# A three-part layer on one core: the prologue in halves with its gate work spread over attention steps, and the first delta-rule head's first stage put ahead of the expert tiles

## The chip, the cores and the metric

One core of one Trainium2 chip runs the whole layer in one launch. The metric is the device time of one execution in microseconds (us). All arithmetic is fp32. The core's engines are PE (matrix multiplies and transposes), DVE and ACT (elementwise work; ACT also has exp, ln and silu, whose tables are loaded when the function changes), POOL (elementwise work and indirect DMAs) and SP, which here only issues DMAs. Each engine runs its own instruction list in order, and they meet through semaphores.

## The reference

Input x has 1024 rows of 256 (two batches of 512). Two branches read the same normalised rows, and both are added to x:

```
xn  = layernorm(x)
out = x + delta(xn) + ffn(xn)

ffn:    h = rmsnorm(xn) * ln1; 16 causal attention heads of 128; hid = xn + attention @ o_w
        x2 = rmsnorm(hid) * ln2; 16 experts, the best 4 for each row, weighted, plus one shared expert
delta:  qkvz = xn @ W_qkvz; ba = xn @ W_ba            (16 key heads, 32 value heads)
        q, k, v = silu(causal convolution of 4 taps); q, k normalised by their lengths
        beta = sigmoid(b);  g = -exp(A_log) * softplus(a + dt_bias);  G = running sum of g in a chunk
        per head: decay = exp(G_i - G_j) below the diagonal; solve a unit triangular system
        from (k k^T) * decay * beta; scan over the chunks; gate with silu(z), rmsnorm, @ W_out
```

## The kernel before

The kernel runs in four sections, in this order on every engine.

**Prologue** (L422 to L480 are SP's and PE's ends of it, L1098 to L1131 ACT's, L1422 to L1470 DVE's). SP loads x in two DMAs that count into one semaphore, and DVE waits for both (L1423). DVE takes the statistics of the eight row tiles (L1424, L1426); ACT takes one square root, DVE a reciprocal, and DVE writes the eight tiles of `xn` (L1431). ACT squares and sums the eight tiles (L1105) and takes a second root (L1107), then copies the transposed rows into `xnT` (L1110). DVE writes the eight scaled tiles `xr` (L1436). PE transposes `xn` (L476), multiplies `xnT` with `W_ba` in 32 small products (L482), transposes `xr` (L489), and DVE copies that to `xrT` with the factor ln1 (L1441). Then the gate work, a chain between DVE, ACT and PE: DVE L1446 to L1450, ACT L1120 to L1124 (exp and ln), DVE L1452 to L1456, PE's sums over a chunk (L573, L574), DVE L1468 and L1470, eight transposes (L577), and ACT's four operations L1127 to L1131, which make `growT` and `erowT`. Mixed into it is the first pair of attention heads: the projections of q and k (L505) and of v (L520). PE starts the scores (L530) only when the gate's sums are there.

**Attention.** 16 steps (eight pairs of heads, twice for the two batches), written out so that PE always has the next pair's projections to do: a step k is v(k), the first two parts of q and k for k+1, transposes of the probabilities of head 0, a third part, transposes for head 1, a fourth, the products with v for both heads (L609), the scores of k+1 for head 0, the output product (L631), the scores for head 1. DVE masks and finds the maxima (L1487, L1489), ACT takes the exponentials (L1157), DVE scales them (L1625). Routing work of the first batch already sits in steps 9, 10 and 12 in the same way, between the two products with v. SP clears 2 MB of the table of rows in each of the first eight steps. `send_rows(0)` on POOL (L1980) scatters the first batch's rows at the end of step 12.

**Shared and routed experts.** PE does six blocks of the shared expert's gate and up products (L647) and six of its down products (L658), DVE the routing in between, and `slots()` (L1589 to L1598) says which tile of 128 rows goes to which expert. POOL scatters the second batch's rows, then adds `hid` to `total` (L1988). Then 47 tiles ("slots") pass one after the other: load the rows, transpose (L684), gate and up (L699), silu and product (L1201, L1674), transpose (L711), down (L720), store. At the end all four engines meet in `section_end` (L270 to L273).

**Delta rule.** After the meeting SP loads the constants and the first weights (L363 to L369), and POOL clears four buffers (L2059 to L2064); PE, ACT and DVE wait for that (L1000, L1345, L1871). The loop over h runs from -2 to 15. Round h holds the scan of head h, the middle stage of head n = h+1 (its triangular system, its values and gates) and the first stage of head f = h+2: keys and queries projected (L749, L759), the convolution's first tap on ACT (L1226) and the other three on DVE (L1704), silu and squares (L1232 to L1249), their sums on PE (L771), lengths and scales on DVE (L1724 to L1739), and the decay table `dec` (SP's rows L376, POOL L1997, L2003 and L2011, ACT L1308). Round -2 has only the first stage of head 0. Round -1 has the first stage of head 1 and the middle stage of head 0, which begins with products of keys (L781) and `MT` (L1748), goes through DRAM (L392 to L401), and solves 16 rows on DVE (L1838 to L1848).

Of the kernel before, what the change touches and what calls it, by code (L numbers as in the profile page):

```python
# [29 lines left out]
RING = 6  # L30
TURN, LOGIT, PLACE = 9, 10, 12
# [12 lines left out]
def build(nc, d, out, debug=None):  # L44
# [9 lines left out]
    with ExitStack() as ctx:  # L54
# [13 lines left out]
        eps6 = sb("eps6", [P, 1])  # L68
        answer = sb("answer", [P, NT, TOPK], mybir.dt.uint32)
        pick = sb("pick", [P, NT, TOPK])  # L70
        yg = sb("yg", [P, 4, H])

# [22 lines left out]
        sd = early("sd", [P, NT])  # L95
        rstd = early("rstd", [P, NT])
        ssq = early("ssq", [P, NT])
        rms = early("rms", [P, NT])
        rrms = early("rrms", [P, NT])
        junk = early("junk", [P, H])  # L100
        eps5 = early("eps5", [P, 1])
        ba = early("ba", [P, NT, 2 * NV])
        ga = early("ga", [P, NT, NV])
        gb = early("gb", [P, NT, NV])
        gc = early("gc", [P, NT, NV])
        gs = early("gs", [P, NT, NV])
        g = early("g", [P, NT, NV])
        G = early("G", [P, NT, NV])

        wqk = early("wqk", [P, 2, HK, 2 * P])  # L110
        wv = early("wv", [P, HK, 2 * P])
        wo = early("wo", [P, 2, H])
# [11 lines left out]
        cmp_b = early("cmp_b", [P, 4, E, E])  # L124
# [40 lines left out]
        w13 = early("w13", [P, SHT, HK, 2 * P])  # L165
        w2 = early("w2", [P, SHT, H])
        sg = early("sg", [P, 2, 512])
        xs = x2[:, 0:RING, :]
        xsT = xrT[:, 0, 0:3 * HK * P].rearrange("p (s k n) -> p s k n", s=3, k=HK)
        sgs = xrT[:, 1, 0:2 * I].rearrange("p (s n) -> p s n", s=2)  # L170
        hs = xrT[:, 1, 2 * I:4 * I].rearrange("p (s n) -> p s n", s=2)
        hsT = early("hsT", [IH, 2, 2, P])
# [17 lines left out]
        gkq = sb("gkq", [P, HK, 2 * D])  # L190
# [4 lines left out]
        cw = sb("cw", [P, NK, 4, TAPS])  # L195
        e_neg = sb("e_neg", [P, P])
        ones = sb("ones", [P, BL])
        cv = sb("cv", [P, 3, B, S])
        kT = sb("kT", [P, 2, NT, P])
        qT = sb("qT", [P, NT, P])  # L200
        sqb = sb("sqb", [P, R, NT, P])
# [3 lines left out]
        dec = sb("dec", [P, R, NT, P])  # L205
# [20 lines left out]
        sst = sb("sst", [P, U, BL])  # L226
        kq2 = sb("kq2", [P, 2, U])
        rk2 = sb("rk2", [P, NT])
        cb = sb("cb", [P, R, 2, NT])
        half = sb("half", [P, 2, U])  # L230
        nk2 = sb("nk2", [P, 2, NT])
        epsq = sb("epsq", [P, 3, NT])
        sxt = sb("sxt", [P, U, BL])
        sxv = sb("sxv", [P, R, NT])
# [44 lines left out]
        def _(sp):  # L279
# [73 lines left out]
            for s in range(RING):  # L353
                load_rows(s)
# [1811 lines left out]
```

## Time and profile before

| | us |
|---|---|
| median of 3 runs | 1630.26 (1629.26 to 1636.0) |
| the profiled execution | 1629.19 |
| its span, first to last instruction | 1627.4 |

| engine | busy us | share of the span |
|---|---|---|
| PE, matrix multiplies | 1534.4 | 94% |
| DVE | 1111.6 | 68% |
| ACT | 784.7 | 48% |
| POOL | 438.4 | 27% |

Busy shares are averages over the whole span. A step inside one section is judged from that section's own rows: who waits there, and for what. "<-" names the releaser of a wait, and times are counted from the span's start.

### The profile page before, as it was taken

To read this page: it belongs to the slowest core of one execution; us is meant where nothing else is said; L and a number is where in the kernel's file an instruction comes from. 1 tells how busy PE (TensorE), PEld (TensorE's weight loads), DVE (VectorE), ACT (ScalarE), POOL (GpSimd) and SP (SyncE) were. 2 spreads that over 40 slices of the span, in tenths; PEclk is the share of its full clock that TensorE was granted. 3 is DMA by queue.
4 is the path that set the end of the run, shared out by engine and by line. 5 is a ranking of instruction groups with operands and counts; after the bars stand their busy time and mean duration, and the time that the engine had idled before them with its cause. 6 is when DMAs were issued, how large, how long until landed. Compare 5 with 4: busy or idle time off the path is not lost.

```text
span 1627.4 us, 29153 instructions
## 1 busy us (share of the span) xinstructions
PE 1534.4 (94%) x10922; PEld 1081.3 (66%) x10922; DVE 1111.6 (68%) x2442; ACT 784.7 (48%) x1692; POOL 438.4 (27%) x277
## 2 busy tenths in 40 slices
PE   4999999999978995699999999999999999999987
PEld 3666666766656773376677677667668668667756
DVE  4544445465362333769889889988988988888875
ACT  3444345343413433445646645646555565564641
POOL 0000000003031005226335344444532531532410
PEclk8999999999998997889999999999999999999999
DMA  3234333223323323323234144143233223323201
GB/s 97 82 116 143 131 115 104 62 70 117 87 99 108 107 85 119 90 63 82 60 99 91 46 103 103 42 100 98 60 72 82 64 65 84 69 57 88 59 11 33
DMA packets 225051, 136.88 MB, mean 84 GB/s; under 512 B 160976, under 2 KB 196304, under 8 KB 224912
## 3 DMA queue, kind: packets, MB, share of 16 engines
q1 hardware_dynamic: 221840, 126.62, 28.6%
q0 software_dynamic: 3072, 8.39, 1.6%
q8 instruction: 89, 1.46, 0.4%
q14 instruction: 50, 0.41, 0.1%
HBM read 94.85 MB, written 35.91 MB: 80 GB/s over the span
## 4 chain that ended last, share of the span: by engine, by line
PE 80%; issue 10%; DVE 5%; ACT 2%; POOL 1%; DMA 1%; POOLq 1%; SPq 0%; ACTq 0%; DVEq 0%
PE ps L912 7%; PE ps L811 7%; PE ps L505 6%; PE ps L830 6%; PE ps L609 4%; PE ps L530 4%; PE ps L631 3%; PE ps L520 3%; PE ps L749 3%; PE ps L851 3%; PE ps L882 3%; PE ps L759 3%; PE ps L861 2%; PE ps L881 2%; PE ps L838 2%
## 5 line engine op out<-in xcount | busy, mean ns | idle before, releaser
L1279 ACT ACTIVATE vs<-ps 128x256 f32<-128x256 f32 x128 | 49.1, 383 | 258.0 <-PE ps L851 253.7
L2027 POOL TENSOR_TENSOR qg<-qT,Ebc 128x1024 f32<-128x1024 f32 x32 | 74.9, 2360 | 357.2 <-PE ps L882 357.2
L1704 DVE SCALAR_TENSOR_TENSOR cv<-ps,cw,cv 128x1022 f32<-128x1022 f32 (+2 forms) x96 | 122.6, 1279 | 28.0 <-ACT cv L1226 24.2
L912 PE MATMUL ps<-wout,xT 128*128 128x256 f32 x512 | 128.8, 396 | 2.2 <-DVE total L1814 2.2
L811 PE MATMUL ps<-xnT,gv 128*128 128x512 f32 x256 | 120.4, 614 | 10.6 <-DVE cv L1704 10.1
L1487 DVE TENSOR_TENSOR ps<-ps,causal_neg 128x128 f32<-128x128 f32 x128 | 37.4, 292 | 131.8 <-PE ps L530 131.8
L1715 DVE SCALAR_TENSOR_TENSOR cv<-ps,cw,cv 128x1022 f32<-128x1022 f32 (+2 forms) x96 | 122.6, 1277 | 5.5 <-ACT cv L1258 3.1
L1814 DVE SCALAR_TENSOR_TENSOR total<-ps,rr,total 128x256 f32<-128x256 f32 x256 | 119.0, 481 | 9.8 <-POOL rr L2033 3.0
L830 PE MATMUL ps<-xnT,gz 128*128 128x512 f32 x256 | 122.8, 604 | 2.6 <-DVE MT L1748 2.4
L505 PE MATMUL ps<-xrT,wqk 128*128 128x512 f32 x256 | 119.5, 601 | 3.6 <-ACT we L1116 2.8
L1157 ACT ACTIVATE we<-ps,bias 128x128 f32<-128x128 f32 (+3 forms) x128 | 65.7, 525 | 106.0 <-DVE bias L1491 106.0
L912 PEld LDWEIGHTS ps<-wout,xT 128*128 128x128 f32 x512 | 93.3, 192 | 28.2 <-issue 12.6
L2011 POOL TENSOR_TENSOR dec<-dec,cb 128x1024 f32<-128x1024 f32 x32 | 60.0, 1896 | 165.5 <-DVE cb L1737 134.5
L811 PEld LDWEIGHTS ps<-xnT,gv 128*128 128x128 f32 x256 | 47.1, 194 | 84.5 <-issue 71.5
L882 PE MATMUL ps<-AT,vs 128*128 128x128 f32 x512 | 91.2, 275 | 0.0
L1969 POOL TENSOR_SCALAR mean<-ssq 128x4 f32<-128x4 f32 x2 | 0.4, 192 | 307.9 <-ACT junk L1141 307.9
L851 PEld LDWEIGHTS ps<-vs,PT 128*128 128x128 f32 x512 | 65.9, 192 | 26.1 <-issue 15.7
L1226 ACT ACTIVATE cv<-ps,cw 128x1024 f32<-128x1024 f32 x32 | 35.6, 1114 | 94.0 <-PE ps L759 62.0
L1997 POOL TENSOR_TENSOR dec<-dec,e_neg 128x1024 f32<-128x1024 f32 x32 | 75.3, 2372 | 15.6 <-DMA dec<-grow_dram 15.6
L505 PEld LDWEIGHTS ps<-xrT,wqk 128*128 128x128 f32 x256 | 46.7, 193 | 45.9 <-issue 40.3
L1782 DVE SCALAR_TENSOR_TENSOR St<-St,eg,ps 128x128 f32<-128x128 f32 x128 | 35.9, 342 | 57.0 <-PE ps L861 57.0
L881 PE MATMUL ps<-qg,St 128*128 128x128 f32 x384 | 74.4, 275 | 0.0
(256 smaller groups left out, 3612.4 us busy)
## 6 DMA issues: line engine op xcount, KB each, us to landing
xs_dram<-zeros SPq DMA_DIRECT2D x16, 1024.0 KB, 6.4
dec<-grow_dram SPq DMA_DIRECT2D x32, 512.0 KB, 4.8
Ebc<-erow_dram SPq DMA_DIRECT2D x32, 512.0 KB, 5.0
wqk<-in_wqk SPq DMA_DIRECT2D x16, 512.0 KB, 3.6
xn<-xs_dram SPq DMA_DIRECT2D x47, 128.0 KB, 2.1
ys_dram<-yg SPq DMA_DIRECT2D x47, 128.0 KB, 1.9
we<-in_we SPq DMA_DIRECT2D x16, 352.0 KB
wv<-in_wv SPq DMA_DIRECT2D x16, 256.0 KB, 3.3
```

Source lines behind the costliest of these rows:

```text
L505: last = mm(ps[:, 6 + j % 2, :], wqk[:, i, c, w * P:(w + 1) * P], xrT[:, c, at:at + S], start=(c == 0), stop=(c == HK - 1))
L811: last = mm(ps[:, (Y, X)[r] + b, :], gv[:, k, r * D:(r + 1) * D], xnT[:, k, b * S:(b + 1) * S], start=(k == 0), stop=(k == HK - 1))
L830: last = mm(ps[:, X + b, :], gz[:, k, r * D:(r + 1) * D], xnT[:, k, b * S:(b + 1) * S], start=(k == 0), stop=(k == HK - 1))
L851: last = mm(ps[:, b, r * D:(r + 1) * D], PT[:, r * NT + 4 * b + m, :], vs[:, r, 4 * b + m, :], start=True, stop=True)
L881: mm(dst, St[:, m % 2, b * R + r, :], qg[:, r, t, :], start=True, stop=False)
L882: last = mm(dst, vs[:, r, t, :], AT[:, h % 2, r, t, :], start=(m == 0), stop=True)
L912: last = mm(ps[:, output_bank(t), r * H:(r + 1) * H], xT[:, r, t * P:(t + 1) * P], wout[:, r, :], start=True, stop=True)
L1704: ins = stt(row, pair(bank)[:, :, 0:S - k], cw[:, f, i, TAPS - 1 - k:TAPS - k], row, ALU.mult, ALU.add)
L1715: ins = stt(row, pair(bank)[:, :, 0:S - k], cw[:, n, 2 + r, TAPS - 1 - k:TAPS - k], row, ALU.mult, ALU.add)
L1814: ins = stt(total[:, t, :], ps[:, output_bank(t), r * H:(r + 1) * H], rr2[:, r, t:t + 1], total[:, t, :], ALU.mult, ALU.add)
L1997: tt(dec[:, r], dec[:, r], e_neg[:].unsqueeze(1).broadcast_to([P, NT, P]), ALU.add).then_inc(fl["g_self"], 1)
L2027: tt(qg[:, r], qT[:], Ebc[:, r], ALU.mult).then_inc(fl["g_qg"], 1)
```

## The change

It has two parts, in one kernel.

**Part one, the prologue.** x's two halves have semaphores of their own, and each half is normalised by itself. The square roots and reciprocals become a power of -0.5 on POOL over four numbers at a time; the mean square of `xn` is computed from the variance (three small DVE operations) in place of ACT's eight squares. `xr` of the first half is turned first, and the first q and k projections follow; the second half's transposes come between them and the next two projections. DVE and ACT share the copies to `xrT`. v(0) moves into step 0. All gate work leaves the prologue: the products with `W_ba` go into step 1 between the two products with v, DVE's and ACT's parts at the end of steps 1 and 2, the sums into step 3, the transposes and the tables into step 4. `growT` is now copied by DVE and `erowT` is taken from it. SP stores both tables in step 5.

**Part two, the first stage of head 0.** `cw`, `e_neg` and head 0's key weights are loaded in the prologue. `dec` of head 0 is loaded in step 6, masked by POOL behind `send_rows(0)`, and its exponential stands on ACT behind step 13. Keys and queries are projected after the last gate and up block (into banks 0 to 3), ahead of the last three down blocks; ACT's and DVE's work on them stands between the shared expert and the slots, `key_squares(0)` ahead of the first slot's transposes, `scaled_decays(0)` and `key_norms(0)` on POOL behind its addition to `total`. The delta-rule loop starts at h = -1. The wait for the cleared buffers is left to SP's `blocks_back(0)`. Some buffers share memory with others than before.

```
@@ SP
-            for i in range(2):
-                dma(total[:, 4 * i:4 * i + 4, :], xv[:, 4 * i:4 * i + 4, :]).then_inc(sm["s_x"], 16)
+            dma(total[:, 0:4, :], xv[:, 0:4, :]).then_inc(sm["s_x"], 16)
+            dma(total[:, 4:8, :], xv[:, 4:8, :]).then_inc(sm["s_x2"], 16)
...
+            for t, n in ((cw, "cw"), (e_neg, "e_neg")):
+                dma(t[:], d[n]).then_inc(fl["d_k"], 16)
+            dma(gkq[:], d["gkq"][0]).then_inc(fl["d_kq"], 16)
...
-                if k == 0:
-                    sp.wait_ge(sm["s_gate_a"], 8)
+                if k == ROWS + 1:
+                    sp.wait_ge(sm["s_gate_a"], 7)
+                    sp.wait_ge(sm["s_gate_v"], 7)
...
+                if k == ROWS + 2:
+                    sp.wait_ge(sm["s_st"], 32)
+                    decay_rows(0)
...
-            consts = ((cw, "cw"), (e_neg, "e_neg"), (normw, "normw"), (U1s, "eye_hi"), (Pb, "eye16"))
-            dma(gkq[:], d["gkq"][0]).then_inc(fl["d_kq"], 16)
+            consts = ((normw, "normw"), (U1s, "eye_hi"), (Pb, "eye16"))
...
@@ PE
+            pe.wait_ge(sm["s_trXE"], 2)
+            project_qk(0, 0, 2)
+            pe.wait_ge(sm["s_xn"], 2 * NT)
+            pe.wait_ge(sm["s_trE"], 2)
+            turn_halves(xr, 1, 0)
+            project_qk(0, 2, 4)
+            pe.wait_ge(sm["s_trE"], 4)
             pe.wait_ge(sm["s_trXE"], 4)
...
             for k in range(B * PAIRS):
-                if k:
-                    project_v(k)
+                project_v(k)
...
+                    if i == 0 and k == GATE:
+                        gate_products()
+                    if i == 0 and k == CUM:
+                        gate_sums()
+                    if i == 0 and k == ROWS:
+                        gate_rows()
...
+                if k == GATE:
+                    pe.wait_ge(sm["s_gate_v"], 1)
+                if k == CUM:
+                    pe.wait_ge(sm["s_gate_v"], 6)
+                if k == ROWS:
+                    pe.wait_ge(sm["s_gate_v"], 7)
...
             gate_and_up(5)
+            pe.wait_ge(sm["f_act"], 5)
+            for b in range(B):
+                project_keys(0, b)
+            pe.wait_ge(sm["f_act"], 6)
+            for b in range(B):
+                project_queries(0, b)
             pe.wait_ge(sm["r_rows"], 5)
             for u in range(SHT, 2 * SHT):
                 down(u)
...
             experts = [expert_of(s) for s in range(3)]
+            key_squares(0)
             turn_slot(0)
...
-            pe.wait_ge(fl["g_zero"], 4)
-            for h in range(-2, NK):
+            for h in range(-1, NK):
@@ ACT
+                if k == ROWS:
+                    exp_rows()
+                if k == GATE:
+                    gate_exps()
+                if k == CUM:
+                    sum_exps()
...
+                if k == PLACE + 1:
+                    early_decays()
...
+            take_key(0, 1)
+            take_key(0, 0)
+            silu_key(0)
+            squares(0, 0)
+            silu_query(0)
+            squares(0, 1)
@@ DVE
+            normalise(0)
+            normalise(1)
+            scale(0)
             dve.wait_ge(sm["s_const"], 48)
+            take_turned(0, 4)
+            scale(1)
+            take_turned(1, 0)
...
+            add_shared(0)
+            add_shared(1)
+            slots()
+            dve.wait_ge(fl["d_k"], 16 * 2)
+            convolve_keys(0, 1)
+            convolve_keys(0, 0)
+            add_shared(2)
+            add_shared(3)
+            answers()
+            key_lengths(0)
+            key_scales(0)
@@ POOL
+            for i in range(4):
+                pool.wait_ge(sm["s_stat"], i + 1)
+                rows = slice(i % 2 * 4, i % 2 * 4 + 4)
+                pool.tensor_tensor((rstd, rrms)[i // 2][:, rows], spread[:, i // 2, rows], minus_half[:],
+                                   ALU.pow).then_inc(sm["s_root"], 1)
...
             send_rows(0)
+            pool.wait_ge(fl["d_k"], 16 * 2)
+            pool.wait_ge(sm["s_prob"], 8 * (ROWS + 1))
+            masked_decays(0)
+            relative_decays(0)
             row_scales(1)
             send_rows(1)
             pool.wait_ge(sm["f_hid"], 4)
             pool.tensor_tensor(total[:], total[:], hid[:], ALU.add)
+            scaled_decays(0)
+            key_norms(0)
             section_end(pool)
```

## Rows read from the trace of the kernel before

**Rows 1.** Windows: length, busy us (instructions) by engine, TensorE clock, DMA share, GB/s.
```profile
20.00:31.00 11.00, 10.07 (x48) 9.67 (x48) 3.61 (x7) 0.20 (x1) 0.00 (x0) 0.53 0.00 0
60.00:85.00 25.00, 25.00 (x103) 16.84 (x103) 11.45 (x33) 10.86 (x33) 0.00 (x0) 1.00 0.44 142
492.00:500.00 8.00, 5.65 (x18) 3.65 (x19) 0.34 (x1) 1.62 (x5) 1.75 (x1) 0.59 0.37 115
```
**Rows 2.** Chain of waits, start us, us: last step of the prologue, first probability transposes.
```profile
48.92 0.88 PE ps L530 x4
...
56.01 0.17 DVE bias L1491
...
58.81 1.28 PE ps L597 x10
```
**Rows 3.** The landing of x's two DMAs (answer for line 284).
```profile
DMA to landing us min/median/max: 4.2/4.7/5.2
```
**Rows 4.** Timeline of the prologue: start us, busy us, engine, line, operation, count.
```profile
6.47 3.65 DVE L1424 BATCH_NORM_STATS2 stats<-total 128x6 f32<-128x256 f32 x8 [6.47 <-DMA total<-in_x]
...
12.76 2.67 DVE L1431 TENSOR_SCALAR xn<-total,mv,rstd 128x256 f32<-128x256 f32 x8
...
20.25 6.66 PE L482 MATMUL ps<-wba,xnT 128*128 128x64 f32 x32 [2.35 <-ACT xnT L1110]
...
31.16 3.70 PE L505 MATMUL ps<-xrT,wqk 128*128 128x512 f32 x8 [0.84 <-DVE xrT L1441]
...
35.39 1.28 ACT L1124 ACT_TABLE_LOAD   x1
...
47.87 1.05 PE L577 MATMUL ps<-ident,G 128*32 128x128 f32 x8 [0.52 <-DVE G L1468]
```
**Rows 5.** Timeline of attention steps: ACT's waits before exponentials of heads 0 and 1.
```profile
97.69 0.37 ACT L1157 ACTIVATE we<-ps,bias 128x128 f32<-128x128 f32 x1 [3.53 <-DVE bias L1491]
...
103.30 0.37 ACT L1157 ACTIVATE we<-ps,bias 128x128 f32<-128x128 f32 x1 [3.47 <-DVE bias L1491]
...
387.29 0.96 POOL L1980 DMA_INDIRECT xs_dram<-xn,place  x1 [0.30 <-issue]
...
445.31 1.04 POOL L1971 TENSOR_TENSOR rr<-mean,minus_half 128x4 f32<-128x4 f32 x1
```
**Rows 6.** Timeline between the shared expert and the first slots.
```profile
480.03 2.46 DVE L1667 TENSOR_TENSOR hid<-ps,hid 128x512 f32<-128x512 f32 x4
...
489.24 4.51 POOL L1988 TENSOR_TENSOR total<-total,hid 128x2048 f32<-128x2048 f32 x1
...
493.74 0.69 PE L684 MATMUL ps<-ident,xn 128*128 128x128 f32 x2 [14.56 <-DMA xn<-xs_dram]
...
498.46 0.34 DVE L1674 TENSOR_TENSOR xrT<-ps,xrT 128x176 f32<-128x176 f32 x1 [13.47 <-ACT xrT L1201]
```
**Rows 7.** Timeline of the delta rule's first rounds.
```profile
616.75 1.80 POOL L2060 MEMSET PT<- 128x2048 f32 x1 [123.00 <-ACTq L272]
...
628.25 7.73 DVE L1704 SCALAR_TENSOR_TENSOR cv<-ps,cw,cv 128x1022 f32<-128x1022 f32 x6 [13.98 <-ACT cv L1226]
...
639.01 1.93 PE L771 MATMUL ps<-sqb,ones 128*32 128x512 f32 x8 [8.69 <-ACT sqb L1249]
...
640.88 2.57 PE L781 MATMUL ps<-kT 128*128 128x128 f32 x16
...
646.26 1.23 DVE L1748 TENSOR_TENSOR MT<-ps,dec 128x1024 f32<-128x1024 f32 x1 [0.56 <-POOL dec L2011]
...
656.00 0.38 DVE L1838 COPY blkT<-blk 128x256 f32<-128x256 f32 x1 [6.25 <-DMA blk<-mt_dram]
```
**Rows 8.** Timeline of the solve in round -1, POOL beside DVE.
```profile
659.80 4.66 POOL L1997 TENSOR_TENSOR dec<-dec,e_neg 128x1024 f32<-128x1024 f32 x2 [7.14 <-DMA dec<-grow_dram]
659.90 2.35 DVE L1844 TENSOR_TENSOR Tprod<-Pb,blkT 128x81 f32<-128x81 f32 x1
```
**Rows 9.** DMA issues from 610 to 700 us: KB each, median us from issue to landing.
```profile
wout<-in_wout SPq DMA_DIRECT2D x1, 256.0 KB, 6.2
```

More of the change, by code:

```diff
@@ new lines, in _, with gate_products @@
+            pe.wait_ge(sm["s_const"], 48)
+            for n in range(2):
+                pe.wait_ge(sm["s_xn"], 4 * n + 4)
+                turn_halves(xn, n, 2 * n)
+            pe.wait_ge(sm["s_xn"], NT + 4)
+            turn_halves(xr, 0, 4)
+            def gate_products():
+                for t in range(NT):
+                    for k in range(HK):
+                        last = mm(ps[:, 0, t * 2 * NV:(t + 1) * 2 * NV], xnT[:, k, t * P:(t + 1) * P], wba[:, k, :],
+                                  start=(k == 0), stop=(k == HK - 1))
+                last.then_inc(sm["s_gate_mm"], 1)
@@ new lines, in expert_of, with expert_weights, slot_gate_and_up @@
+            def expert_of(s):
+                return pe.value_load(slot_expert[0:1, s:s + 1], min_val=0, max_val=E - 1)
+            def expert_weights(table, e, k):
+                return table.rearrange("p e (k n) -> p e k n", k=2)[:, bass.DynSlice(e, 1), k, :].rearrange("p e n -> p (e n)")
+            def slot_gate_and_up(s, e):
+                pe.wait_ge(sm["m_xE"], s + 1)
+                if s >= 2:
+                    pe.wait_ge(sm["m_h"], s - 1)
+                for k in range(HK):
+                    last = mm(ps[:, s % 2, 0:2 * I], xsT[:, s % 3, k, :], expert_weights(we13[:], e, k),
+                              start=(k == 0), stop=(k == HK - 1))
+                last.then_inc(sm["m_g"], 1)
@@ L1002, in _ @@
+            section_end(pe)
+            for h in range(-1, NK):
                 n, f = h + 1, h + 2
@@ L1452, in _ @@
-            step(ts(gs[:], gs[:], 1.0, None, ALU.add))
-            step(dve.reciprocal(gs[:], gs[:]))
-            dve.wait_ge(sm["s_gate_a"], 4)
-            step(tt(ga[:], ga[:], gb[:], ALU.add))
-            stt(g[:], ga[:], -1.0, alog[:].unsqueeze(1).broadcast_to([P, NT, NV]), ALU.mult,
-                ALU.mult).then_inc(sm["s_gate_v"], 1)
+            for n in range(2):
+                dve.wait_ge(sm["s_x2" if n else "s_x"], 16)
+                for t in range(4 * n, 4 * n + 4):
+                    last = dve.bn_stats(stats[:, t, :], total[:, t, :])
+                step(last)
+                for t in range(4 * n, 4 * n + 4):
+                    last = dve.bn_aggr(mv[:, t, :], stats[:, t, :])
+                step(last)
+                rows = slice(4 * n, 4 * n + 4)
+                ts(spread[:, 0, rows], mv[:, rows, 1], 1e-5, None, ALU.add).then_inc(sm["s_stat"], 1)
@@ new lines, in normalise @@
+            def normalise(n):
+                dve.wait_ge(sm["s_root"], n + 1)
+                for t in range(4 * n, 4 * n + 4):
+                    ts(xn[:, t, :], total[:, t, :], mv[:, t, 0:1], rstd[:, t:t + 1], ALU.subtract,
+                       ALU.mult).then_inc(sm["s_xn"], 1)
+                rows = slice(4 * n, 4 * n + 4)
+                step(tt(square[:, rows], rstd[:, rows], rstd[:, rows], ALU.mult))
+                step(tt(square[:, rows], square[:, rows], mv[:, rows, 1], ALU.mult))
+                ts(spread[:, 1, rows], square[:, rows], 1e-6, None, ALU.add).then_inc(sm["s_stat"], 1)
@@ L1613, in _ @@
                 score_maxima(k, 1)
[L1614 to L1617 removed]
+                take_v(k)
                 for i in range(2):
```

617 lines of the change are left out of this document (301 added, 316 removed).

## The prediction

> **What bounds the kernel now.** I read the windows first, by section, then the chain of waits, then the timeline at the seams. Inside the attention PE is busy 25.00 of 25.00 us at full clock (1.00, the 2.4 GHz level) [rows 1]: a step there costs what PE does in it, and whatever is added on PE is paid in full. The seams are different. In the prologue PE gets its first real work at 20.25 and runs it at a granted clock of 0.53, near the 1.2 GHz level [rows 1]; the chain reaches the scores at 48.92 and the first probability transposes at 58.81, and from there PE doesn't stop [rows 2]. Between the shared expert and the slots PE waits 14.56 us for scattered rows that come back from DRAM [rows 6]. After the slots the engines meet at 616.75, and the delta rule's first stage runs alone, one operation behind the other: cleared buffers, key products, 7.73 us of convolution, squares, scales, until `MT` is whole at 647.49 (646.26 + 1.23) and its blocks are back from DRAM at 656.00 [rows 7]. So three idle stretches are to be shortened or filled; I price each as a shift of the first point behind it that nothing else sets.
>
> **Prologue, to the first probability transposes.** Of x's two DMAs one took 4.2 us to land and one 5.2 [rows 3]; the second is issued half a us later, so the first half is there at about 4.9, 1.5 us before DVE starts now (6.47, rows 4). Four statistics are half of 3.65 us at most, 1.8 with the wait after each, some 1.5 without them; four aggregates, two waits and the small addition add 0.7. That gives 7.1 for the first half and 9.3 for the second. POOL's power takes 1.04 [rows 5] and is ready at 8.2, under DVE's second half. normalise(0) is half of 2.67 us [rows 4], with three small operations 1.9: 11.2. normalise(1): 13.2. scale(0): 1.1, so 14.3. PE turns eight tiles in about 1.0 (the eight transposes of L577 took 1.05, rows 4), the copy takes 0.65, and q starts at 15.9. Eight passes of 512 columns take 3.70 at full clock [rows 4] and twice that at half. I take half clock for the first four, since PE had only short bursts before, as in the stretch at 0.53 [rows 1]: 5.2, so 21.1. Eight transposes 1.0, eight passes 3.5, ACT's copy 0.5: scores at 26.1. Bounds: all at full clock 24, all at half 32.5.
> From the scores on the order is new too. DVE's maxima for both heads end at 56.01, 7.1 us after the scores began [rows 2]; only then comes the copy of v(0), which now stands in step 0, and the next q and k projections wait for its two halves. So 7.1 + 0.7, then twice four passes of 1.7 or so: the first transposes stand 11.2 behind the scores, where now they stand 9.9 behind them (58.81 - 48.92). PE has v's products (3.5 us) to do under the maxima, so they cost nothing more. 26.1 + 11.2 = 37.3 against 58.81: **-21.5 us** (-23.5 to -15).
>
> **Gate work in steps 1, 3 and 4.** PE's 32 products took 6.66 us at half clock [rows 4]; in a step at full clock they are half, 3.3. The four products of the sums are at most 0.23 us each (3.70 / 16 per 256 columns), 0.9. Eight transposes 1.05. Together **+5.3 us**, with nothing to hide them, since PE is full there. The waits behind them are hidden: PE has the second head's products with v (2.2 us, half of the sixteen passes) between the gate work and its wait, and DVE's copy of `ba`, of the sums or of `growT` is 0.7 to 1.2 us on a DVE that is idle there. ACT's four operations in step 1 and the ln table, with the exp table's return, are two loads of 1.28 [rows 4] and 1.5 of work, 4.0 us against an idle 3.53 before the exponentials of head 0 [rows 5]; the 0.5 left over goes into the 3.47 before head 1's. DVE's 2.9 us in step 2 and ACT's two in step 3 fit in the same way; DVE's `growT` and the tables in step 4, 2.5 us, end about when the scores do. Without this cover each would cost its excess, under 1 us in three steps; bound 0 to +3, I take 0. In step 5 SP's two stores replace those of step 0. In step 6 SP adds 1 MB (two loads) before 2 MB of clearing; the next weights are needed a step of 24.6 us later (DMA share in a step 0.44, rows 1), so nothing. The earlier loads of `cw`, `e_neg` and the key weights stand behind what the prologue needs.
>
> **`dec` on POOL and ACT.** POOL's last scatter of the first batch ends at 388.25 (387.29 + 0.96, rows 5). Behind it come two masks and two relative decays, 4.66 [rows 8] and 3.8: to 396.8, and `row_scales(1)` is due only at 445 [rows 5]. ACT reaches `early_decays` at about 392.4 (step 14's first transposes are at 58.81 + 14 x 24.6 + 3.7 of routing work = 406.9, and the products with v end 14.6 before them), and stands there until the second table is ready: ends 397.9. Queued behind it are step 14's exponentials for head 0, due 4.3 us after the scores begin, at 396.6: 1.3 late, 2.2 long, and the idle 3.47 before head 1's [rows 5] takes it up. Cost 0; if POOL is over 2 us later, PE waits for the excess.
>
> **Between the shared expert and the slots.** PE adds key and query projections, 2 x 3.5 us, before the last down blocks; it stands idle there anyway. DVE's first two additions to `hid` go ahead of `slots()`, which ends at 481.3 where it now ends at 480.03 [rows 6]; SP needs it only at the end of the scatter. The convolution, 7.73 [rows 7], ends at 489.1, the other additions at 490.4. ACT's silu and squares end 2.1 behind the convolution, at 491.3; PE's `key_squares(0)`, 1.93 [rows 7], ends at 493.3, and the first slot's transposes wait for it in PE's queue. They start at 493.74 now, when the rows land [rows 6]: 0.4 to spare. Next late is DVE: `answers()` 2.6, lengths 0.7, scales 0.9 behind 490.4 end at 494.6, well before the first slot product at 498.46 [rows 6], unless DVE is held up.
> It may be. At 659.80 POOL works on `dec`, and a DVE product of 81 elements that starts beside it takes 2.35 us [rows 8], where its neighbours take 0.2: it waits for POOL's operation to end. POOL's addition to `total`, 4.51 us in one instruction [rows 6], would start at 490.4, just when DVE starts `answers()`. Then DVE's products of two SBUF operands wait until 494.9, `answers()` ends at 497.3, and the scales at 499.1, **+0.6 us** for the first slot. Bounds -2 (PE stands shorter at half clock: it was at 0.59 until 500, rows 1) and +4.
> The Trainium skill states this as a rule ("SBUF: State Buffer", section "Who interferes with whom"): a DVE instruction with two SBUF inputs and a GpSimd instruction that reads SBUF exclude each other for the whole instruction. The trace agrees (2.35 us). By the rule the term is the +0.6, without it 0.
>
> **The seam to the delta rule.** At the meeting, `kT`, `qT` and the scaled `dec` exist. PE's key products take 2.57 at mixed clock [rows 7], I take 3.1: 619.9. Two `MT` operations of 1.23 follow [rows 7]: 622.4 against 647.49, **-25.1 us**. PE no longer waits for POOL's clearing (from 616.75, 4.7 us), and only SP's `blocks_back` does, 25 us later. SP issues three constants, gv, gz, wout and the two rows of `Ebc` first, some 3.7 us, so it is ready at 620.9.
> But these are 2.2 MB, and `MT`'s blocks are queued behind them. Now `wout`, the last of 1.6 MB issued over four us, took 6.2 us to land [rows 9]; `Ebc`, 1 MB more, would land near 628.5, and the blocks have to be in DRAM before SP issues their way back, which in an empty queue would be at 627.3 (8.5 us from 647.49 to 656.00 in all). I take 2.1 us for it: the solve starts at 633 against 656.00, **-23.0 us**. Bounds: -25.1 with no queueing, -19 if every byte goes ahead. All of round -1 behind the solve hangs on this chain and moves with it, POOL's masks beside DVE's products included.
> The Trainium skill says ("DMA: Bandwidth & Descriptors", section "Queues, rings and completion order") that each DMA engine consumes the descriptors of a ring in order. By that rule the sum has the 2.1; by free overtaking it would be 2.1 less. The trace of before shows such queueing only in `wout`'s 6.2 us.
>
> **Sum.** -21.5 + 5.3 + 0.6 - 23.0 = -38.6 us. The profiled execution took 1629.19, 1.8 over its span of 1627.4; it would be 1590.6. The median of before is 1.1 above that execution, so 1591.7.
>
> **Rivals.**
> (a) The prologue stays at half clock: its bursts are now shorter and further apart. For it: 0.53 over eleven us of dense small work [rows 1]. Against: eight passes at 31.16 ran at full clock in 3.70 [rows 4]. Scores at 32.5, +6.4: **1598**.
> (b) The queue of loads at the seam takes more, the solve starts at 637: +4 to +5, **1596**. For it the 6.2 us; against, the blocks are small.
> (c) The stage in front of the slots is not hidden: if the convolution's six operations each wait for a scatter's 0.96 us on POOL, DVE is 6 to 8 us later, `key_squares(0)` too, and PE's first slot with it one for one: **1599**. Against: the six run in 7.73, 1.29 each, at 628 [rows 7] with POOL at work beside them; they read PSUM.
> (d) The gate work stalls its steps (ACT's table loads, POOL's lateness in step 14): 3 to 6 us, **1596**. Against: the idle 3.5 us twice per step.
> (e) Slower than before: PE's clock. If the waits in steps 1 to 4 and the thinner prologue leave TensorE at half clock far into the attention, each us at half costs half a us. It decides against the change from 77 us at half clock (38.6 x 2); at 90 us the time is **1637**. Against: once PE is without gaps it is at 1.00 over the whole step [rows 1].
>
> **Chances.** Forecast (1586 to 1595) 0.62, (a) 0.13, (b) 0.10, (c) 0.05, (d) 0.06, (e) 0.02, anything else 0.02. The range 1585 to 1600 takes the forecast, (b), (d), and most of (a) and (c), and its lower end the gains on both clock terms. A difference under 0.5% (8 us) can't be told from none here: faster 0.96, same 0.02, slower 0.02.
>
> **What would show it.** Right: scores at 25 to 28 and the first transposes of probabilities near 37; steps 1, 3 and 4 longer by 3.3, 0.9 and 1.05, the others at 24.6; PE's first slot transposes as long behind the last scatter as now; `MT` whole 5 to 6 us behind the meeting and the solve at 15 to 17. Wrong: idle PE in steps 1 to 4 or 14, a first slot over 2 us later against the scatter, or a solve over 19 behind the meeting.

## The result, and the profile after

The changed kernel took **1594.1 us** in the median of four runs (1593.2 to 1595.5), beside 1630.3 for the kernel before (1629.3 to 1636.0): a ratio of **0.977, interval 0.975 to 0.980**. The forecast was 1591.7, with a range of 1585 to 1600. The profiled execution took 1593.2 us with a span of 1591.4, against 1629.2 and 1627.4: -36.0, where the sum had said -38.6.

First the windows, with the columns of rows 1: the prologue, the last stretch before the first slot product, and the end of the solve of round -1 with the work behind it.

```profile
20.00:31.00 11.00, 10.22 (x37) 6.12 (x36) 5.62 (x18) 4.03 (x11) 0.00 (x0) 1.00 0.16 48
472.00:480.00 8.00, 6.70 (x20) 3.21 (x21) 7.37 (x11) 1.73 (x5) 4.61 (x2) 0.50 0.38 105
620.00:640.00 20.00, 8.01 (x15) 3.20 (x14) 18.60 (x21) 3.29 (x3) 8.23 (x4) 0.69 0.12 18
```

The prologue's stretch was granted 0.53 before [rows 1]; now it is at 1.00, and PE has its scores in it. The timeline of PE there (start, busy us):

```profile
24.22 4.55 PE L552 MATMUL ps<-act_t,we 128*128 128x128 f32 x16 [0.78 <-ACT act_t L1150]
28.61 3.62 PE L542 MATMUL ps<-cv,xrT 128*128 128x256 f32 x16
32.52 3.67 PE L527 MATMUL ps<-xrT,cv 128*128 128x512 f32 x8 [0.29 <-DVE act_t L1563]
36.03 1.25 PE L610 MATMUL ps<-ident,we 128*128 128x128 f32 x10
```

Scores start at 24.22, not 48.92, and the first probability transposes at 36.03, not 58.81 [rows 2]: -22.8. From there I followed the start of one DVE instruction per attention step in both traces. The shift goes from -22.8 to -19.2 after step 1 (the gate's 32 products, 3.52 us in the chain of waits), to -18.4 after step 3 and to -17.5 after step 4, and stays at -17.5 through step 15. So the gate work cost 5.3 us, and nothing stalled.

Then DVE ahead of the slots (POOL's addition to `total` runs from 471.37 for 4.51 us):

```profile
471.20 0.17 DVE L1698 TENSOR_SCALAR shift<-start_of 128x16 f32<-128x16 f32 x1
471.39 4.52 DVE L1699 TENSOR_TENSOR shift<-shift,steps_row 128x16 f32<-128x16 f32 x1
475.95 0.29 DVE L1700 TENSOR_TENSOR row_of<-row_of,shift 128x128 f32<-128x128 f32 x1
```

An addition of 16 elements a partition took 4.52 us: it ended with POOL's instruction, as the forecast had it. The first slot product starts at 479.35 instead of 498.46 [rows 6], a shift of -19.1.

The meeting moved from 616.75 to 597.58 (-19.2). Of the seam, the timeline of DVE, SP's queue and PE, in order of time:

```profile
599.72 2.36 DVE L1809 TENSOR_TENSOR MT<-ps,dec 128x1024 f32<-128x1024 f32 x2 [3.92 <-PE ps L729]
...
602.88 5.04 SPq L402 DMA_DIRECT2D mt_dram<-MT  x4
607.97 4.35 SPq L407 DMA_DIRECT2D MTc<-MT  x4
612.36 1.36 SPq L411 DMA_DIRECT2D blk<-mt_dram  x2
...
616.08 0.38 DVE L1901 COPY blkT<-blk 128x256 f32<-128x256 f32 x1 [11.74 <-DMA blk<-mt_dram]
...
635.55 6.49 PE L759 MATMUL ps<-xnT,gv 128*128 128x512 f32 x8 [11.99 <-DVE cv L1765]
```

`MT` is whole at 602.1, 4.5 us behind the meeting, and the solve starts at 616.08 instead of 656.00 [rows 7], 18.5 behind the meeting where 16.3 was forecast. Note the busy time of SP's first two rows: issuing four DMAs of 64 KB took SP 5.04 and 4.35 us.

### The profile page after: what moved, and what is told of

Read it like the earlier page. It is cut to its first block, busy times and chain, and to the rows that moved or that the text cites. A ratio compares the mean times of both kernels' runs of the same rounds, so it can differ in the third digit from the quotient of the medians.

```text
span 1591.4 us, 29140 instructions
## 1 busy us (share of the span) xinstructions
PE 1529.3 (96%) x10922; PEld 1078.1 (68%) x10922; DVE 1115.5 (70%) x2447; ACT 777.2 (49%) x1672; POOL 442.6 (28%) x279
## 4 chain that ended last, share of the span: by engine, by line
PE 89%; DVE 4%; issue 2%; SPq 1%; DMA 1%; POOL 1%; ACT 1%; POOLq 0%; DVEq 0%; ACTq 0%
PE ps L860 7%; PE ps L759 7%; PE ps L527 7%; PE ps L778 7%; PE ps L622 4%; PE ps L552 4%; PE ps L993 4%; PE ps L656 3%; PE ps L799 3%; PE ps L542 3%; PE ps L830 3%; PE ps L704 3%; PE ps L694 3%; PE ps L1016 3%; PE ps L809 2%
## 5 line engine op out<-in xcount | busy, mean ns | idle before, releaser
L759 PE MATMUL ps<-xnT,gv 128*128 128x512 f32 x256 | 121.5, 618 | 12.5 <-DVE cv L1765 12.0
L527 PE MATMUL ps<-xrT,cv 128*128 128x512 f32 x256 | 117.8, 593 | 1.1 <-ACT xrT L1144 0.8
L759 PEld LDWEIGHTS ps<-xnT,gv 128*128 128x128 f32 x256 | 47.5, 196 | 87.0 <-issue 73.9
L552 PE MATMUL ps<-act_t,we 128*128 128x128 f32 (+3 forms) x256 | 74.2, 433 | 0.8 <-ACT act_t L1150 0.8
L830 PEld LDWEIGHTS ps<-AT,vs 128*128 128x128 f32 x512 | 74.7, 194 | 0.0
```

Source lines behind the costliest of these rows:

```text
L527: last = mm(ps[:, 6 + j % 2, :], wqk[:, i, c, w * P:(w + 1) * P], xrT[:, c, at:at + S], start=(c == 0), stop=(c == HK - 1))
L552: mm(score(i, qt), aqT[:, q:q + P], akT[:, i * S:i * S + (qt + 1) * P], start=True, stop=True).then_inc(sm["s_sc"], 1)
L759: last = mm(ps[:, (Y, X)[r] + b, :], gv[:, k, r * D:(r + 1) * D], xnT[:, k, b * S:(b + 1) * S], start=(k == 0), stop=(k == HK - 1))
L830: last = mm(dst, vs[:, r, t, :], AT[:, h % 2, r, t, :], start=(m == 0), stop=True)
```

## The experiments

There are twelve runs: the two kernels once more, seven with one edit each, and three that put several edits together (`seam_best`, `best`, `sends_later`). The expectations call PE TensorE, DVE VectorE and ACT ScalarE. The later jobs ran on three chips of the same kind (the record doesn't name the first job's), where the kernel before takes 1638 to 1641 us instead of 1630, so I compare ratios to it, and starts within the traces. The changed kernel again:

> The changed kernel itself, unchanged, beside the variants. In the four runs before, TensorE stood still for about 17 us between steps 13 and 14 of attention (from 361 us on where the step was at its new place), which the first profile of the changed kernel does not have, while every other start agreed with it to 0.1 us. Theory (a property of the chip that the job falls on, for whatever kernel): either this run and all its neighbours have the stall or none has, and the ratio to the kernel before stays near 0.98. Rival (a property of the variants): this run has none, ratio 0.977, and its neighbours have it.

Measured: 1601.2 us beside 1640.0, ratio 0.978 (0.976 to 0.979), so the gain holds. The standstill is in this run too, so it isn't a property of the variants alone. But it is smaller (the start of step 15 slips by 8.1 us; in the run `mtc_behind` below by 17.8), which the theory doesn't explain; the rows below do.

**Part two undone.**

```
-            pe.wait_ge(sm["f_act"], 5)
-            for b in range(B): project_keys(0, b)
...                                (also queries, squares, ACT's, DVE's and POOL's parts)
             section_end(pe)
+            for b in range(B): project_keys(0, b)
```

> Against the changed kernel (1594.1 us): the first stage of delta rule head 0 stands behind the meeting again, the new prologue and the gate work inside the attention steps stay. My theory, two parts that add up: MT whole comes about 25 us later than 4.5 us behind the meeting, and the seam gives back the roughly 4.2 us that the blocks of MT lost behind the 2.2 MB of loads (their DMA issues took 5.04 + 4.35 us), and the slots give back 0.6: 25.1 - 4.2 - 0.6 = +20.3, so about 1614 (1611 to 1618). Rival (the gain came mostly from the prologue, and the stage in front of the slots is paid for by the slots): +15 or less, 1609. The solve starts 40 us behind the meeting, and the half clock stretch at 627 moves with it.

Measured: 1626.8, ratio 0.990 (0.989 to 0.992), 17.4 us over its neighbours `ebc_behind` and `mtc_behind` (1609.3 and 1609.6), which equal the changed kernel but for the seam. By the starts, head 1's `MT` comes 18.2 us later. Of the standstill in attention this run has 1.4 us less than `mtc_behind`, and its prologue is 0.5 longer; counted from step 15 on it is 19.1. So the stage in front of the slots is worth 17 to 19 us, a little less than the 20.3. The seam's queueing is shown by what is not there when the loads have 25 us to drain; SP's issues and the solve of this run:

```profile
642.61 1.97 SPq L402 DMA_DIRECT2D mt_dram<-MT  x4
644.62 2.78 SPq L407 DMA_DIRECT2D MTc<-MT  x4
...
651.30 0.38 DVE L1895 COPY blkT<-blk 128x256 f32<-128x256 f32 x1 [6.46 <-DMA blk<-mt_dram]
```

The solve starts 8.7 us behind whole `MT` (642.6), against 14.0 in the changed kernel.

**Gate work in one piece, ahead of the first scores.**

```
             pe.wait_ge(sm["s_trXE"], 4)
+            gate_products(); gate_sums(); ...; gate_rows()
             scores(0, 0)
```

> Against the changed kernel: all gate work (32 products, sums, row transposes and what VectorE and ScalarE do between them) stands in one piece ahead of the first scores, instead of in attention steps 1, 3 and 4. Theory: TensorE saves the 5.3 us in the steps and pays the whole chain once: 3.5 + 0.9 + 0.9 us of TensorE and about 8 us of small VectorE and ScalarE instructions and waits between them, so the first probability transposes come 12 to 14 us later (36.0 to about 49) and the end 7 to 9 us later: about 1602. Rival (before's prologue lost its time to the half clock and to its serial halves, not to the gate work): the chain hides beside project and scores, +0 to +3, 1596. If the idle time in the chain drops the granted clock, another 3 to 6 us: 1606.

Measured: 1623.4, ratio 0.989 (0.987 to 0.990), 14 us over the same neighbours: more than my worst case of 12. PE's timeline:

```profile
23.98 3.68 PE L496 MATMUL ps<-wba,xnT 128*128 128x64 f32 x32
34.02 1.19 PE L505 MATMUL ps<-qT,cum_mask 128*128 128x256 f32 x2 [6.36 <-DVE qT L1535]
...
40.24 7.18 PE L552 MATMUL ps<-act_t,we 128*128 128x128 f32 x16 [1.30 <-DVE cmp_a L1548]
```

The chain costs 16.0 us before the scores (40.24 - 24.22), and the granted clock falls to 0.50 from 30 to 45, so the scores take 7.18 instead of 4.55. The first probability transposes are 18.1 late, and from step 5 on it is 12.8, once the steps without gate work have given 5.3 back. Of the net gain of part one, 17.5 us, taking the gate chain out of PE's way is thus the larger share, 12.8, and halves and POOL's powers are the other 4.7. (An upper bound for the chain: the kernel before covered a part of it with projections.)

**The loads ahead of the blocks of `MT`.**

```
-                    exponential_rows(n)
+                    if n: exponential_rows(n)
                     blocks_out(n)
+                    if n == 0: exponential_rows(n)
```

> For head 0 alone the two broadcast loads of exponential rows (1 MB written) are issued behind the ten block DMAs of MT instead of ahead of them. Queue theory: the issues of the block DMAs (5.04 and 4.35 us for four each, against 1.97 and 2.78 in the kernel before) stall because the queue is full of bytes; without 1 MB of them they shrink and the blocks land earlier: solve start 2 to 5 us nearer to the meeting than 18.5 us, total 1589 to 1592. Rival (only issue order counts): 0.9 us, the two issues themselves: 1593.2. Second rival: Ebc late (last_exponentials and decayed queries on POOL) costs nothing, as POOL is idle there; if it does, +1.

The solve now starts 9.0 us behind whole `MT` instead of 14.0. The queue theory holds: -5.0, not 0.9. But the end of the stretch didn't move: from whole `MT` of head 0 to the start of head 1's it is 62.5 us here and 62.6 in `after_again`. (The total, 1609.3, ratio 0.981 with 0.979 to 0.983, says less: the changed kernel itself wasn't run in this job, and the standstill in attention is 9.7 us longer here than in `after_again`.) SP's queue, then what the trace shows inside the solve:

```profile
620.71 2.18 SPq L402 DMA_DIRECT2D mt_dram<-MT  x4
622.93 3.16 SPq L407 DMA_DIRECT2D MTc<-MT  x4
...
629.68 0.38 DVE L1904 COPY blkT<-blk 128x256 f32<-128x256 f32 x1 [6.73 <-DMA blk<-mt_dram]
...
634.12 4.67 POOL L2143 TENSOR_TENSOR qg<-qT,Ebc 128x1024 f32<-128x1024 f32 x2
...
634.13 2.46 DVE L1910 TENSOR_TENSOR Tprod<-Pb,blkT 128x100 f32<-128x100 f32 x1
636.91 2.02 DVE L1910 TENSOR_TENSOR Tprod<-Pb,blkT 128x121 f32<-128x121 f32 x1
639.28 2.02 DVE L1910 TENSOR_TENSOR Tprod<-Pb,blkT 128x144 f32<-128x144 f32 x1
```

The solve took 18.5 us instead of 15.1. It lies beside seven operations of POOL and not four; six of its products are held off, for 11.7 us where they need 2. The edit itself brought POOL's first three there: they need `Ebc`, whose landing now lets them start at 633.95, where in the changed kernel POOL had done them from 610.47 to 615.29, before the solve began. So the second rival was there too, and cost more than its 1 us. Of the queue's 5.0 us POOL took 3.4; why the other 1.6 didn't reach head 1's `MT` no run shows.

**The gathers ahead of the copies.** In `blocks_out`, for every head:

```
+                for w in range(2): dma(blk[...], ...)
                 for q in range(4): dma(MTc[rows], MT[rows, :, rows])
-                for w in range(2): dma(blk[...], ...)
```

> In every head the two gathers of diagonal blocks (blk) are issued right after mt_dram has landed, ahead of the four copies of MT into MTc, which now follow them. In the seam the four MTc issues take 4.35 us between the last mt_dram issue (607.9) and the blk issues (612.4). Theory: mt_dram lands before those are done, so the issues themselves are on the path: solve start up to 4.35 us earlier, total 1590. Rival: mt_dram is late anyway (median landing 6.2 us after issue, so the last at about 613): SP would only wait in the same place, 0 to -1 us, 1593.5. In the scan heads nothing changes, since the solve has slack there; if MTc comes too late for the first blocks of T, each head pays: slower.

The solve starts 13.0 us behind `MT` instead of 14.0, total 1609.6, ratio 0.981 (0.978 to 0.984): the rival's answer, SP waits for `mt_dram` in the same place.

**POOL silent until the solve is over.**

```
                     decayed_queries(n)
+                if h == -1:
+                    pool.wait_ge(fl["v_base"], 1)
                 if ahead:
                     masked_decays(f)
```

> POOL's two masked and two relative decay operations for head 1 wait until VectorE has solved the 16-row blocks of head 0. In the changed kernel four of VectorE's products in that solve took 2.26, 2.01, 1.67 and 1.57 us where their neighbours of nearly the same size took 0.23 to 0.34, and they lie at the starts of POOL's operations of 2.3 and 1.9 us; in the kernel before the same four took 2.35, 2.02, 1.66 and 1.57. Theory (POOL's operations on SBUF hold VectorE's off): 7.5 - 1.1 = 6.4 us off the solve, all on the path to the values of head 0, so the scan of head 0 starts 6 us earlier and the total falls by 5 to 6.4 against the changed kernel. Rival 1: the products are slow for themselves (their size, or TensorE's half clock): 0. Rival 2: POOL's work, later by 9 us, then holds off VectorE's convolutions or ScalarE's decays instead: 0 to -2.

Measured: 1596.3 beside 1601.2 for the changed kernel in the same job, ratio 0.975 (0.972 to 0.978). The medians are 5 us apart but the intervals of the two ratios overlap, so the trace has to decide: from whole `MT` of head 0 to the start of head 1's it is 56.7 us instead of 62.6, -5.9, and the solve takes 8.7 instead of 14.9. It is the theory, and rival 1 falls: the same product of 81 elements takes 0.24. The convolutions beside POOL's masks still take 7.71 for six, so rival 2 falls too.

**All seam edits together.**

```
-            dma(gv[:], d["gv"][0]); dma(wout[:], d["wout"][0])
...
                     blocks_out(n)              (gathers ahead of the copies)
+                    if n == 0: exponential_rows(n); dma(gv...); dma(wout...)
...
+                if h == -1: pool.wait_ge(fl["v_base"], 1)
                 if middle: decayed_queries(n)
```

> Four edits of the seam together: for head 0 the loads of exponential rows, of the value weights and of the output weights are issued behind the block DMAs of MT; the gathers of diagonal blocks go ahead of the copies into MTc; and all of POOL's work of that round (decayed queries too) waits for the end of the solve. The run with the exponential rows alone behind had the solve start 9.0 us behind MT whole instead of 14.0, but then six of VectorE's products took 1.6 to 2.5 us and the solve ended where it would have anyway. Theory: solve start at 8 us behind MT whole, no product held off (-6.4 us), total 11 to 12.5 us under the changed kernel. Rival: POOL's work, now 13 us behind the solve, holds off the six convolution operations of the next keys (1.28 us each): half of it comes back, -5. Second rival: value weights or MTc late for TensorE: -8.

Two parts of this hadn't run alone: the loads of `gv` and `wout` behind the blocks, and POOL's wait ahead of `decayed_queries` too. Measured: **1587.3**, ratio 0.968 (0.966 to 0.970), 13.9 under the changed kernel in the same job. DVE's rows in the solve:

```profile
622.68 0.38 DVE L1904 COPY blkT<-blk 128x256 f32<-128x256 f32 x1 [5.18 <-DMA blk<-mt_dram]
626.58 0.25 DVE L1910 TENSOR_TENSOR Tprod<-Pb,blkT 128x81 f32<-128x81 f32 x1
...
631.43 0.37 DVE L1914 COPY Tt<-Pb 64x256 f32<-64x256 f32 x1
```

The solve starts 7.4 us behind `MT` (14.0 in the changed kernel), nothing is held off, and from `MT` to the next head's `MT` it is 51.3 us against 62.6: -11.3, as expected. POOL's 13 us behind the solve hold off nothing.

**POOL's addition to `total` behind its other work.**

```
-            pool.tensor_tensor(total[:], total[:], hid[:], ALU.add)
             scaled_decays(0)
             key_norms(0)
+            pool.tensor_tensor(total[:], total[:], hid[:], ALU.add)
```

> POOL's add into total (4.5 us on 128x2048) goes behind its scaled decays and key norms, so it lies in the first expert tiles instead of beside VectorE's answers. Theory (POOL holds VectorE off): VectorE's 128x16 addition that took 4.52 us takes 0.2, key scales end 4.3 us earlier, and the first slots, which waited for VectorE about 0.5 us, start 0.5 us earlier; but the slots' own VectorE products lie beside the add then: if they are held off too (they read PSUM and are 0.34 us long), up to 2.3 us come back: -0.5 to +2 against the changed kernel. Rival (no such hold): nothing moves, 0.

The rows of DVE and POOL:

```profile
486.54 0.18 DVE L1699 TENSOR_TENSOR shift<-shift,steps_row 128x16 f32<-128x16 f32 x1
...
495.50 4.53 POOL L2183 TENSOR_TENSOR total<-total,hid 128x2048 f32<-128x2048 f32 x1
```

The addition takes 0.18 instead of 4.52. From step 15 to the twenty-fifth slot it is 126.8 us, against 127.4 in the changed kernel of this job: -0.6. But in the nine other profiles in which this stretch has the same code it takes 126.7 to 129.0, so the -0.6 isn't shown; what is shown is that DVE isn't held. The slots' own products (one operand in PSUM) aren't held off either. The total, 1605.9, ratio 0.980 (0.979 to 0.982), is 4.7 higher all the same: in its trace 2.1 us more standstill in attention, 1.0 more in the prologue and 1.2 more behind the last `MT`, none of it near the edit.

**The standstill in attention.** This I hadn't looked for. Where the profile of the first job runs through, all later ones stop. PE's timeline in the first one, then in `mtc_behind`, both behind the v products of step 13:

```profile
357.74 3.62 PE L542 MATMUL ps<-cv,xrT 128*128 128x256 f32 x16
361.19 3.60 PE L527 MATMUL ps<-xrT,cv 128*128 128x512 f32 x8
364.62 1.25 PE L610 MATMUL ps<-ident,we 128*128 128x128 f32 x10
```

```profile
357.74 3.62 PE L542 MATMUL ps<-cv,xrT 128*128 128x256 f32 x16
362.75 1.95 PE L527 MATMUL ps<-xrT,cv 128*128 128x512 f32 x4 [1.40 <-DVE act_t L1563]
369.73 3.78 PE L527 MATMUL ps<-xrT,cv 128*128 128x512 f32 x4 [5.03 <-DVE act_t L1563]
379.66 2.37 PE L610 MATMUL ps<-ident,we 128*128 128x128 f32 x10 [6.14 <-DVE we L1719]
```

Meanwhile POOL issues its 16 scattering DMAs (350 to 370). DVE and SP both see the v products done 7.6 us later than in the first profile, and it is 17.8 us before step 15 in that run. The last wait, 6.14 us for DVE's scaling of the probabilities, has a cause that its rows show:

```profile
369.80 9.71 DVE L1719 TENSOR_SCALAR we<-we,prec 128x128 f32<-128x128 f32 x4
370.51 4.64 POOL L2110 TENSOR_TENSOR dec<-dec,e_neg 128x1024 f32<-128x1024 f32 x2
375.23 4.00 POOL L2116 TENSOR_TENSOR dec<-dec,gates 128x1024 f32<-128x1024 f32 x2
```

Four scalings that take 1.28 us elsewhere take 9.71 beside POOL's decay work for head 0, which part two of the change put behind the scatter. In the first profile they were over at 364.9 and the decay work began at 370.8; late by the first delay, they meet. This parts the twelve later profiles: in the six in which scalings meet the decay work (`stage_back`, `gate_front`, `ebc_behind`, `mtc_behind`, `seam_best`, `add_last`) the slip is 10.2 to 17.8 us, in the other six 5.9 to 8.1. So the standstill is two things: a first delay of 6 to 8 us, and up to 10 more that the change's own decay work adds. No run moves the decay work alone.

> The kernel before, for its profile on this chip. It ran at 1630 us in the first job and at 1640 in the two jobs since. Theory: the same standstill of TensorE that the profiles of the variants show beside POOL's 16 scattering DMAs (step 12 to 14 of attention, 8 to 17 us) is in it too, here at about 370 to 395, and explains the 10 us. Rival: it has none and is slower for another reason.

1640.1, ratio 1.000 (0.9985 to 1.002), and the standstill is there: from step 12 to step 15 it is 80.6 us, where the first profile has 74.7. So the first delay comes with the job, for either kernel. It is 5.9 of the 13.1 us by which this profile is longer than the first one; 1.7 lie in the prologue, 5.5 behind step 15. PE's timeline, behind the v products of that step:

```profile
382.07 1.89 PE L505 MATMUL ps<-xrT,wqk 128*128 128x512 f32 x4
387.56 2.49 PE L505 MATMUL ps<-xrT,wqk 128*128 128x512 f32 x4 [3.60 <-DVE act_t L1462]
```

The load of an expert's weights moved one step later, out of the scatter:

```
-                else:
+                elif k != PLACE:
                     load_expert(k - 8)
+                if k == PLACE + 1: load_expert(PLACE - 8)
```

> The changed kernel with the load of one expert's weights (528 KB, issued at 356 us, in the middle of POOL's 16 scattering DMAs, which run from 350 to 370) moved one step later, to about 381 us. Theory (the standstill at 361 comes from the load and the scatter meeting in the DMA engines): it goes or shrinks to under 3 us; 5 to 12 us off the changed kernel's time on the same chip. Rival (the scatter alone, or where the instructions of that step lie): it stays at 8 us or more, and the time is the changed kernel's, ratio 0.977 to the kernel before.

1601.6, ratio 0.977 (0.975 to 0.979). The standstill stays, 7.6 us between steps 12 and 15 against 8.1 in `after_again` on another chip, and 5.9 in `before_again` on the same one, whose load isn't moved: my theory falls, the load isn't it.

Both together, the seam edits and this one:

> The four seam edits (block DMAs of MT ahead of the loads, gathers ahead of the copies, POOL silent until the solve is over) together with the expert load one step later. Seam alone measured 13.9 us under the changed kernel in medians, and 11.2 by the starts in the trace. If the load theory holds, 16 to 24 under it (1577 to 1585 where the changed kernel is at 1601), ratio to the kernel before 0.961 to 0.966; if not, the seam's 11 to 14 us alone, ratio 0.968 to 0.970.

1587.8, ratio 0.9685 (0.967 to 0.970): the seam's gain alone, as the second case had it.

Last, the seam edits with the scatter moved instead:

```
+            pool.wait_ge(sm["s_prob"], 8 * (ROWS + 1)); masked_decays(0); relative_decays(0)
             row_scales(0)
+            pool.wait_ge(sm["s_prob"], 8 * 15)
             send_rows(0)
```

> The four seam edits, and POOL's 16 scattering DMAs of the first half (350 to 370 us, steps 12 and 13 of attention) held back until the probabilities of step 14 are there (about 388), with its decay work of head 0 moved ahead of them (to about 185 us). Moving the expert load away had left the standstill as it was (7.9 us). Theory (the scatter alone makes TensorE stand still): the standstill moves with it, to about 390 to 410, and the starts of steps 13 and 14 agree with the profile of the changed kernel that had none; time as with the seam edits alone, ratio 0.968. Rival (a place of the program in step 13, whatever POOL does): the starts slip by 4 and then 4 us at the same steps as before. Third case (the scatter there is harmless, as the scatter of the second half beside the shared expert looks): no standstill, ratio 0.961 to 0.964. The decay work beside attention may hold VectorE off for up to 4 us once; the trace shows it at 185.

1593.0 (1587.8 to 1600.1), ratio 0.974 (0.972 to 0.976). The standstill has moved with the scatter, which now starts at 393.13 and ends at 413.3; PE's row there:

```profile
413.81 6.39 PE L545 MATMUL ps<-cv,xrT 128*128 128x256 f32 x16 [3.37 <-DVE hid L1599]
422.48 2.81 PE L613 MATMUL ps<-ident,we 128*128 128x128 f32 x13 [2.27 <-DVE we L1722]
```

Steps 13 and 14 start as regularly as in the first profile (365.6 and 390.2), and step 15 is 6.3 us late. The decay work beside attention cost 3.4 us at 212 to 221, once, as I had feared. Here the scalings of that step meet no decay work, and the slip is of the smaller size. So the first delay goes with the scatter, at both places where it lay, and the version is no gain. What it is in the scatter stays open (its descriptors, its 1 KB packets, the semaphores): no run takes these apart. Why the first job shows nothing is open too.

The best version measured is the seam edits alone or with the load moved, 0.968 of the kernel before and 0.991 of the changed one (1587.3 beside 1601.2 in one job).

## Why the prediction was right, by its own steps

- **Prologue**, -21.5 forecast, -22.8 measured. The order of releases was right; the term mis-sized was the clock of the first q passes, taken at half (5.2 us). The stretch was granted 1.00, and scores came at 24.2, where the bound for full clock was 24 (and the sign of being right 25 to 28). The first transposes stood 11.8 us behind them, not 11.2, which took 0.6 of that back.
- **Gate work**, +5.3 forecast and measured: 3.6 in step 1, 0.9 each in steps 3 and 4. PE was full, so instructions times duration was the whole truth, and rival (d) didn't come. `gate_front` shows the alternative, 16 us in front of the scores.
- **`dec` on POOL and ACT**, 0: steps 13 to 15 don't move in the first pair of profiles. But the reason given was incomplete: it looked at ACT's queue and at PE, and not at DVE, whose scalings the same POOL operations hold off where they meet. In `sends_later` that cost 3.4 us in step 8, and in the six later profiles named above it is part of a slip of 10.2 to 17.8. The 0 holds only where step 13 isn't late.
- **Slots**, +0.6 forecast by way of a product held off from 490.4 to 494.9. It was held off for 4.52, but the cost for the slots isn't shown: `add_last` differs by 0.6, less than profiles of the same code do. In the first profiles the shift goes from -18.9 at the shared expert to -19.1 at the first slot; PE is at half clock for 10.2 us there, against 17.1 before, which may hide it.
- **Clock**, no term of the sum. A stretch at half clock in step 15 (20 transposes, 4.04 us before and 2.68 after) gave 1.4.
- **Seam**, -23.0 forecast, -20.75 measured (-39.92 against -19.17). `MT` was whole 4.5 us behind the meeting, 1.1 sooner than forecast. The queueing was mis-sized: 2.1 taken, 5.3 measured (14.0 against 8.7 with the queue empty). I had priced a late landing; SP's own issues stretched as well, from 1.97 + 2.78 to 5.04 + 4.35 us [the rows of `stage_back` and of after], and `blk` is issued behind all eight. Rival (b) had 20.3 behind the meeting; the measured 18.5 is halfway to it, and outside the 15 to 17 that were the sign of being right.
- **Behind the solve**, 0 forecast. The eight passes of L759 took 6.49 at mixed clock, and 1.2 came back by the first scan head; then the shift stays at -38.7 to head 15. Behind that 2.7 are lost at half clock in the tail: 17 us at half, against 11. In the changed kernel's second profile the tail is at half for 10 and 1.8 us shorter, so this term varies with the execution.

Sum: -22.8 + 5.3 - 1.4 - 0.3 - 20.75 + 1.2 + 2.7 = -36.0. The total was closer than its terms: the prologue gave 1.3, the clock in step 15 1.4 and the slots 0.9 that I hadn't counted, while the seam took 2.3 and what lies behind the solve 3.9. That these nearly cancel is luck; the mechanisms of the prologue, the gate work and the seam are not.

## What to carry to other kernels

A step that moves ahead of a barrier leaves its transfers behind: list what the issuing queue has in front of them at their new time, and put the small transfers that a chain waits for ahead of the large ones that have time. When a start moves, look at who works beside it then: of five us won in a queue another engine took 3.4 at once, and the queue's edit paid only together with that engine's silence. The same holds for work placed where its engine is idle: POOL's decay work cost nothing in the first profiles, and up to 10 us when the step beside it came late. Work whose results are due late is worth a wait, if the engine it would hold off is on the path.

## What the runs showed of the hardware

- DVE's products of two SBUF operands don't run beside a POOL operation on SBUF. One of 16 elements took 4.52 us beside POOL's 4.51, 0.18 elsewhere; products of 81 to 225 elements took 1.6 to 2.5 instead of 0.25 to 0.4. Operations with one operand in PSUM aren't touched: six convolutions take 7.71 us with POOL at work or silent. The Trainium skill states this ("SBUF: State Buffer", section "Who interferes with whom"), and these traces agree. The kernel before had 6.4 us of it in its first solve, in four products, of which [rows 8] has the first. An operation with a single SBUF tile as input can be held too: DVE's scalings of the probabilities by a column, in SBUF, took 9.71 us for four beside POOL's decay work (`mtc_behind`), 1.28 elsewhere.
- Issuing a DMA is not of one price. Four of 64 KB took SP 1.97 us with an empty queue (`stage_back`), 2.18 behind 1.2 MB (`ebc_behind`), and 5.04 behind 2.2 MB (the first profile).
- Beside sixteen scattering DMAs of POOL (128 rows of 1 KB each) a step of PE came 5.9 to 8.1 us late in six profiles, and 10.2 to 17.8 in six more, in which POOL's decay work held DVE off too. In the two profiles of the first job nothing was late. The cause of the first part is open.
